# Decoder of four layers on one core: a memory region of its own for the per-token head attention, its score products in two halves, first loads and all items in another order

## The chip, the cores and the metric

The kernel runs on one core of one Trainium2 chip. The metric is the device time in microseconds (us) of one execution of the whole program. The engines are PE (TensorE, matrix products), DVE (VectorE), ACT (ScalarE), POOL (GpSimd) and SP (SyncE, which here issues all DMAs). Each works through its own list of instructions in order, and they wait for one another by semaphores.

## What is computed

A decoder of four layers with layer norm after each of its twelve stages, on x of 4 batches x 512 tokens x 128 features and a context of 154 tokens. All is float32 at the interface.

```python
x = _layernorm(x + L0_attn(x))            # 16 heads of 8, rotary, causal            stage L0a
x = _layernorm(x + L0_xattn(x, ctx))      # cross attention, 154 keys                L0x
x = _layernorm(x + L0_ffn(x))             # quantised to 8 bit, depthwise conv, silu ffn0
x = _layernorm(x + L1_attn(x))            # heads1, see below
x = _layernorm(x + L1_xattn(x, ctx, mask))#                                          L1x
x = _layernorm(x + L1_ffn(x))             # 16 experts, best two of each token       moe1
x = _layernorm(x + L2_attn(x))            # rotary, causal                           L2a
x = _layernorm(x + L2_xattn(ctx, x, mask))#                                          L2x
x = _layernorm(x + L2_ffn(x))             # 128-512-512-512-128                      ffn2
x = _layernorm(x + L3_attn(x))            # one head, distance bias                  self3
x = _layernorm(x + L3_xattn(x, ctx))      # causal                                   L3x
x = _layernorm(x + L3_ffn(x))             # 8 experts, weighted                      moe3
```

`heads1` is unusual: each token attends over its own 16 heads, not over other tokens. For each token, 16 x 16 scores are products of 8-element vectors of its query and key, a softmax runs over them, and they weigh the token's 16 value vectors of 8.

## The kernel before

Everything stays in on-chip memory with features on the partitions (`XT`, 128 x 4 x 512). The work is cut into **items**, each a (kind, stage.batch, number): `project`, `max`, `split`, `turn`, `pair`, `value`, `copy`, `out`, `mix` for the attentions with 16 heads (in two passes: `max` computes scores for the row maxima, `pair` computes them again, transposed, for exp), stage kinds such as `q0x`, `h0`, `h0t`, `h0b` (ffn0), `qkv`, `hs`, `hv`, `hm`, `ht` (heads1), `ew`, `gu`, `dn`, `acc` (experts), and the tail `wo`, `square`, `mean`, `x` that ends each stage of each batch (output product, layer norm, new x). There are 2338 items. A hand-written table `STEPS` gives the order of kinds, and three lists (`FRONT_ORDER`, `SIDE_ORDER`, `TAIL_ORDER`) the order of batches within a kind. Every engine walks through the same list `PLAN` and issues its part of each item, so the table sets the order on all five engines at once. Nothing is moved at run time: an engine whose next instruction waits does not go on to later ones.

The stages that are no 16-head attention ("side" stages: ffn0, heads1, moe1, ffn2, self3, moe3) all keep their working data in one region, `SIDE` (128 x 6656 floats). `side_free` makes the first item of each user wait for the last read of the one before, in `SIDE_ORDER`. So heads1 of a batch can't begin before ffn0 of the batch ahead of it in that list has ended, and the next ffn0 or moe1 not before `ht` of heads1.

A heads1 batch has four quarters of 128 tokens. For each, PE multiplies (`qkv`, L987), ACT copies (L1748), and DVE does `hs`: a product of 128 x 2048 elements (L1395, into `PR1`), a sum of eights (L1399), the maxima (L1400) and the subtraction (L1401). ACT takes exp (L1752). POOL does `hv`: four products of 128 x 512 (L1937, into `PV1`). DVE does `hm`: sum and reciprocal (L1405, L1406), a sum over `PV1` (L1408) and the scaling (L1409). There is one `PV1`, so `hv` of a quarter waits for `hm` of the quarter before. 

The start: SP loads the first half of the weights (`pack`), x of batch 0, the rotary tables, the constants (`STAGE`, 2496 columns), 18 small fixed rows, x of batches 1 to 3 in one transfer (L1982), then batch 0's queries and keys, which go out to DRAM (`scratch`, L2010, L2014) and come back with another layout (`QH`, `KH`, L2025). The three bf16 pieces of batch 0's queries are made by DVE (L1212 to L1216), those of its keys by POOL (L1874 to L1879). DVE casts the mask columns of the constants (L1173, in `base_setup`), and SP copies them with halves swapped into `CS` (L1988, `swap_halves`). The first `max` product on PE (L824) needs `QH`, `KH` and `CS`.

Other buffers that the change touches: `OK0` and `OK1` (normalised outputs, L1292), `OT` (turned back, the operand of `wo`), `YT` (the same for the experts), `RS0` and `RS1` (the reciprocal deviation, L1715).

## Time and profile before

| | us |
|---|---|
| median of 3 runs | 1685.9 (1683.88 to 1687.15) |
| the profiled execution, its own time | 1692.29 |
| span in its profile | 1690.6 |
| PE busy | 1359.3 (80% of the span) |
| DVE busy | 1084.9 (64%) |
| ACT busy | 736.6 (44%) |
| POOL busy | 372.9 (22%) |

Busy time is the time in which an engine has an instruction under way. Its share of the whole span says little by itself, since the stages differ: the same engine can be full in one stretch and wait in another. So the profile is read by stretches, and in each by what the waiting engines wait for. "PEclk" is the share of full TensorE speed that the chip granted: 1.00 stands for 2.4 GHz, 0.50 for 1.2 GHz.

### The profile page before, as it was taken

How to read it: one execution, taken by the hardware profiler on the slowest of the kernel's cores; microseconds unless marked ns; L12 is line 12 of the kernel's file. 1: busy time of each engine (PE TensorE's matmuls, PEld its weight loads, DVE VectorE, ACT ScalarE, POOL GpSimd, SP SyncE). 2: the span in 40 equal slices, each digit the busy share in tenths (PEclk: the TensorE clock that was granted, in tenths of full speed). 3: DMA queues.
4: the chain of work that ended last, by engine and by line, in shares of the span. 5: the costliest groups of instructions: out<-in, count | busy, mean ns of one | idle time of the engine just before them, and what ended most of it. 6: DMA issues, size and time to landing. Idle time of an engine off the chain costs nothing.

```text
span 1690.6 us, 25807 instructions
## 1 busy us (share of the span) xinstructions
PE 1359.3 (80%) x9530; PEld 648.6 (38%) x9530; DVE 1084.9 (64%) x2336; ACT 736.6 (44%) x1035; POOL 372.9 (22%) x475
## 2 busy tenths in 40 slices
PE   3476878886566676677678999899999999979986
PEld 1133433332232242244233545444444444445443
DVE  3466677887668758768987667666234624267765
ACT  1027556754323412322446653346755545435542
POOL 2214235103303312610943012022211010011000
PEclk8559899987666797799779999999999999989989
DMA  6520224200020030123113123230211321022111
GB/s 161 131 58 12 49 39 103 46 1 2 0 38 2 20 83 11 47 62 63 40 39 72 49 67 77 44 98 30 64 38 39 77 63 63 2 61 67 40 38 49
DMA packets 50072, 86.35 MB, mean 51 GB/s; under 512 B 13718, under 2 KB 42198, under 8 KB 45526
## 3 DMA queue, kind: packets, MB, share of 16 engines
q1 hardware_dynamic: 49950, 84.71, 21.7%
q8 instruction: 78, 1.28, 0.3%
q14 instruction: 44, 0.36, 0.1%
HBM read 66.95 MB, written 15.60 MB: 49 GB/s over the span
## 4 chain that ended last, share of the span: by engine, by line
PE 54%; DVE 20%; DMA 7%; ACT 6%; issue 5%; POOL 4%; SPq 4%; ACTq 0%; DVEq 0%; POOLq 0%
PE ps L897 6%; PE ps L1051 6%; PE ps L824 6%; DVE MX L1261 5%; PE ps L1017 5%; PE ps L1024 4%; PE ps L1018 4%; POOL SIDE L1937 3%; PE ps L830 3%; PE ps L735 3%; PE ps L782 3%; PE ps L858 2%; DMA SIDE<-in_experts 2%; SPq L2025 2%; ACT WORK L1683 2%
## 5 line engine op out<-in xcount | busy, mean ns | idle before, releaser
L1261 DVE TENSOR_REDUCE MX<-ps 128x3 f32<-128x462 f32 (+5 forms) x704 | 411.7, 626 | 158.0 <-PE ps L830 136.5
L1683 ACT ACTIVATE WORK<-ps 128x1024 f32<-128x1024 f32 (+1 forms) x352 | 318.8, 945 | 164.3 <-PE ps L858 122.7
L824 PE MATMUL ps<-KH,QH 48*128 48x154 bf16 (+5 forms) x1536 | 142.4, 271 | 104.5 <-DVE MX L1261 63.2
L897 PE MATMUL ps<-WORK,VA 128*18 128x512 f32 (+3 forms) x1536 | 165.7, 518 | 20.8 <-ACT WORK L1683 14.9
L1923 POOL TENSOR_SCALAR_AFFINE_SELECT WORK<-WORK 128x256 f32<-128x256 f32 (+1 forms) x192 | 95.1, 503 | 337.3 <-ACT WORK L1683 336.7
L1777 ACT ACTIVATE SIDE<-ps 128x512 f32<-128x512 f32 x96 | 57.1, 597 | 252.3 <-PE ps L1018 252.2
L1937 POOL TENSOR_TENSOR SIDE<-SIDE 128x512 f32<-128x512 f32 x64 | 113.6, 1806 | 240.3 <-ACT SIDE L1752 210.8
L824 PEld LDWEIGHTS ps<-KH,QH 48*128 48x128 bf16 (+1 forms) x1536 | 59.1, 96 | 268.2 <-DVE MX L1261 156.2
L1507 DVE TENSOR_TENSOR SIDE<-SIDE,ps 128x512 f32<-128x512 f32 x96 | 65.5, 686 | 109.1 <-ACT SIDE L1777 107.8
L858 PE MATMUL ps<-QH,KH 54*128 54x512 bf16 (+3 forms) x768 | 118.0, 352 | 19.8 <-ACT WORK L1683 17.9
L1017 PE MATMUL ps<-XT,SIDE 128*128 128x512 f32 x192 | 112.1, 668 | 20.1 <-DMA SIDE<-in_experts 19.8
L1024 PE MATMUL ps<-SIDE 128*128 128x128 f32 x768 | 110.1, 290 | 18.4 <-DVE SIDE L1507 14.9
L1024 PEld LDWEIGHTS ps<-SIDE 128*128 128x128 f32 x768 | 97.6, 198 | 49.4 <-issue 36.2
L1518 DVE SCALAR_TENSOR_TENSOR SIDE<-ps,SIDE 128x128 f32<-128x128 f32 x352 | 98.8, 343 | 18.5 <-PE ps L1024 16.5
L1018 PE MATMUL ps<-XT,SIDE 128*128 128x512 f32 x192 | 102.5, 616 | 0.0
L1876 POOL CAST HQ<-WORK 128x512 bf16<-128x512 f32 x23 | 16.0, 694 | 379.7 <-DVE WORK L1248 379.3
L782 PE MATMUL ps<-XT,pack 128*128 128x512 f32 x96 | 66.0, 796 | 23.2 <-DMA XT<-in_xT 14.5
L735 PE MATMUL ps<-pack,SIDE 128*128 128x128 f32 x260 | 50.9, 342 | 27.9 <-DVE SIDE L1384 10.3
L858 PEld LDWEIGHTS ps<-QH,KH 54*128 54x128 bf16 x768 | 33.7, 97 | 98.4 <-ACT WORK L1683 54.7
L1626 ACT ACT_TABLE_LOAD x38 | 48.8, 1283 | 30.2 <-PE ps L858 7.6
L946 PE MATMUL ps<-SQ,pack 128*128 128x512 f32 x96 | 55.1, 657 | 7.7 <-ACT SQ L1705 7.3
L897 PEld LDWEIGHTS ps<-WORK,VA 128*18 128x18 f32 x1536 | 30.2, 98 | 75.8 <-issue 29.2
(279 smaller groups left out, 2182.9 us busy)
## 6 DMA issues: line engine op xcount, KB each, us to landing
SIDE<-in_experts SPq DMA_DIRECT2D x96, 192.0 KB, 2.4
scratch<-HQ SPq DMA_DIRECT2D x48, 192.0 KB, 2.9
QH<-scratch SPq DMA_DIRECT2D x48, 192.0 KB
SIDE<-in_wide SPq DMA_DIRECT2D x8, 1024.0 KB, 6.2
QH<-scratch SPq DMA_DIRECT2D x48, 128.0 KB
scratch<-HK SPq DMA_DIRECT2D x16, 192.0 KB, 3.0
QH<-scratch SPq DMA_DIRECT2D x48, 64.0 KB
KH<-scratch SPq DMA_DIRECT2D x16, 192.0 KB
```

Of the source, the lines that this page charges most:

```text
L735: mm = pe.transpose(bank[:, t * 128:t * 128 + 128], src, eye)
L782: mm = pe.matmul(bank[:, 0:src.shape[1]], w, src, start=True, stop=True)
L824: mms[b] = pe.matmul(banks[b][:, c * pitch:c * pitch + width], qr[b][:, h, t * 128:t * 128 + 128], kr[b][:, h, 0:width], start=(c == 0), s ...
L858: mm = pe.matmul(bank[:, b, q0 * (len(hs) == 1) + i * (S - q0):][:, 0:S - q0], kr[b][:, h, kt * 128:kt * 128 + 128], qr[b][:, h, q0:S], st ...
L897: mm = pe.matmul(ps[32 * j:32 * j + 2 * NV, UB, q0:S], lhsT.rearrange("p a c -> p (a c)"), PB[:, (PAIR_BASE[F] + where[pi]) % NSLOT, b, at ...
L1017: pe.matmul(banks[:, 0, :], gates(key, i)[:, 0:128], XT[:, b, :], start=True, stop=True)
L1018: pe.matmul(banks[:, 1, :], gates(key, i)[:, 128:256], XT[:, b, :], start=True, stop=True).then_inc(all_wide, 1)
L1024: mm = pe.matmul(bank[:, t * 128:t * 128 + 128], HID[n % 2][:, t * 128:t * 128 + 128], gates(key, i)[:, 256:384], start=True, stop=True, s ...
L1051: mm = pe.matmul(bank, hidden(l, k, c), src[:, k, :], start=(k == 0), stop=(k == FC - 1))
L1261: dve.tensor_reduce(MX[:, 32 * b + i0:32 * b + i0 + cnt], src, AX.X, ALU.max, negate=True).then_inc(freed, 1)
L1683: act.activation(PB[:, N % NSLOT, :, lo:hi], wide_banks("pair", F, n)[:, :, lo:hi], ACT.Exp).then_inc(sem("exp_done"), 1)
L1937: pool.tensor_tensor(out[:, hs], SC1[i][:, hs].unsqueeze(2).broadcast_to([128, n_heads, DH, H]), v.broadcast_to([128, n_heads, DH, H]), AL ...
```

## The change

1. **A region for heads1.** `SIDE` shrinks to 5160 columns, and a new region `HEADS` (3840 columns) holds `PV1`, `QKV1`, `SC1` and `OH1`. `PR1` and two small vectors lie in `pack`, over weights of L0a and L0x that are no longer read by then (with waits for it). heads1 leaves `SIDE_USERS` and has a list of its own, so it and ffn0 or moe1 may run at the same time. `SIDE_ORDER` becomes ... heads1.0, ffn0.2, heads1.1, ffn0.3, heads1.2, moe1.0, heads1.3, moe1.1 ...
2. **Score products in halves.** `PR1` has 1024 columns in place of 2048: product and sum of eights are done for heads 0 to 7, then for 8 to 15.
3. **Memory for it.** One `OK` in place of two, `OT` in place of `YT`, the exponential of L1715 written over `SQ` in place of `RS`. The waits follow (`JOINED`).
4. **First loads.** x of batch 1 in a transfer of its own, before the constants; of the constants only the 1088 mask columns, the other 1408 later with the rest; the keys' pieces of batch 0 on DVE (`split_first`); the cast of the masks right behind it; `swap_halves` between the loads of `QH` and `KH`.
5. **Order.** All of `STEPS` is new. `TAIL_ORDER` and `FRONT_ORDER` stay.

```diff
-ffn0.0 ffn0.1 heads1.0 ffn0.2 ffn0.3 heads1.1 moe1.0 heads1.2 moe1.1 heads1.3 moe1.2 moe1.3 ffn2.0 ffn2.1 self3.0
+ffn0.0 ffn0.1 heads1.0 ffn0.2 heads1.1 ffn0.3 heads1.2 moe1.0 heads1.3 moe1.1 moe1.2 moe1.3 ffn2.0 ffn2.1 self3.0
-project*5 pieces project*5 send base max*2 pieces max*2 project max*4 project max*2 project max*3 project send max*2
+project*5 pieces send base project*5 max*2 pieces max*2 project max project max*5 project max*2 project max*2 send max
...
-        SIDE = sb("SIDE", [128, 6656])
+        SIDE, HEADS = sb("SIDE", [128, 5160]), sb("HEADS", [128, 3840])
...
-        OK = [sb(f"OK{i}", [128, QT, D]) for i in range(2)]
+        OK = sb("OK", [128, QT, D])
...
-        OT, YT = sb("OT", [128, S]), sb("YT", [128, S])
-        YC, SQ, RS = ([sb(f"{n}{i}", [128, S]) for i in range(2)] for n in ("YC", "SQ", "RS"))
+        OT = sb("OT", [128, S])
+        YC, SQ = ([sb(f"{n}{i}", [128, S]) for i in range(2)] for n in ("YC", "SQ"))
...
-        PR1, PV1 = side(0, 2048), side(2048, 2048)
+        _products = AT["L0a.wq"][0]
+        PR1, PV1 = pack[:, _products:_products + 1024], heads(0, 2048)
...
+        def heads_free(eng, key):
+            n = HEADS_USERS.index(key)
+            if n == 0:
+                consumed(eng, "rest", 0)
+                eng.wait_ge(sem("masks_ready"), 3)
+            if n:
+                filled(eng, "ht", HEADS_USERS[n - 1])
...
                 if kind == "hs":
-                    link(dve.tensor_tensor(p, qs.unsqueeze(2).broadcast_to([128, H, H, DH]),
-                                           ks.unsqueeze(1).broadcast_to([128, H, H, DH]), ALU.mult))
-                    link(dve.tensor_reduce(SC1[i], p, AX.X, ALU.add))
+                    for at in (0, HH):
+                        hs = slice(at, at + HH)
+                        link(dve.tensor_tensor(p, qs[:, hs].unsqueeze(2).broadcast_to([128, HH, H, DH]),
+                                               ks.unsqueeze(1).broadcast_to([128, HH, H, DH]), ALU.mult))
+                        link(dve.tensor_reduce(SC1[i][:, hs], p, AX.X, ALU.add))
...
                     if key == 0 and i == 1:
-                        split_queries()
+                        split_first(TQ, TRQ, HQ, (0, 1, 2), 1, "queries_split")
+                    if key == 0 and i == 3:
+                        split_first(TK, TRK, HK, (2, 1, 0), 3, "keys_split")
+                        first_masks()
...
-            sp.dma_start(STAGE, d["const"]).then_inc(sem("const_loaded"), 16)
+            sp.dma_start(XT[:, 1:2, :], d["xT"][:, 1:2, :]).then_inc(sem("x_loaded1"), 16)
+            sp.dma_start(STAGE[:, 0:NMASK], d["const"][:, 0:NMASK]).then_inc(sem("const_loaded"), 16)
...
-            sp.dma_start(XT[:, 1:B, :], d["xT"][:, 1:B, :]).then_inc(sem("x_loaded1"), 16)
+            sp.dma_start(XT[:, 2:B, :], d["xT"][:, 2:B, :]).then_inc(sem("x_loaded2"), 16)
```

Where the order moves instructions. **The start, on SP** (its list of DMAs; `QH` and `KH` are batch 0's operands, `CS` the swapped masks, `pack` at 4569 columns the second half of all weights). Before:

```order
L2025 DMA QH<-scratch 8x4096 x2
L2025 DMA KH<-scratch 24x4096 x2
L2025 DMA KH<-scratch 16x4096 x2
L2025 DMA KH<-scratch 8x4096 x2
L1963 DMA CT<-in_cT 128x640
L1964 DMA pack<-in_pack 128x4569
L1965 DMA SIDE<-in_mask_q 128x640
L1966 DMA SIDE<-in_mask_k 128x512
L1967 DMA SIDE<-in_mask_k 32x512
L1968 DMA SIDE<-in_mask_c 128x640
L1969 DMA mconst<-in_mconst 3x1
L1988 DMA CS<-const 64x1088 x2
```

Now:

```order
L2052 DMA QH<-scratch 8x4096 x2
L2015 DMA CS<-const 64x1088 x2
L2052 DMA KH<-scratch 24x4096 x2
L2052 DMA KH<-scratch 16x4096 x2
L2052 DMA KH<-scratch 8x4096 x2
L1988 DMA CT<-in_cT 128x640
L1989 DMA pack<-in_pack 128x4569
L1990 DMA SIDE<-in_const 128x1408
```

The copy into `CS` has moved from behind the load of `pack` to ahead of the loads of `KH`.

**heads1 of batch 2, on DVE.** Before, it begins when moe1 of batch 0 has ended (L1524 is that stage's `acc`, L1273 to L1276 the `split` of L1x.1):

```order
L1524 TENSOR_TENSOR YT<-ps,XT 128x512
L1261 TENSOR_REDUCE MX<-ps 128x2 x2
L1273 CAST MP<-MX 128x2x4x8
L1274 TENSOR_TENSOR MR<-MX,MP 128x64
L1275 CAST MP<-MR 128x2x4x8
L1276 TENSOR_TENSOR MP<-MR,MP 128x2x4x8
L1395 TENSOR_TENSOR SIDE<-SIDE 128x2048
L1399 TENSOR_REDUCE SIDE<-SIDE 128x256
L1400 TENSOR_REDUCE SIDE<-SIDE 128x16
L1401 TENSOR_TENSOR SIDE<-SIDE 128x256
```

Now its second quarter stands between experts of moe1.0 (L1527 is `gu`, L1536 and L1538 are `dn`, L1242 belongs to L1x.1's last projection):

```order
L1527 TENSOR_TENSOR SIDE<-SIDE,ps 128x512
L1536 TENSOR_SCALAR SIDE<-ps,SIDE 128x128 x4
L1242 TENSOR_TENSOR VR<-ps,BLOCKS 128x2x8x8
L1538 SCALAR_TENSOR_TENSOR SIDE<-ps,SIDE 128x128 x4
L1527 TENSOR_TENSOR SIDE<-SIDE,ps 128x512
L1417 TENSOR_TENSOR pack<-HEADS 128x1024
L1419 TENSOR_REDUCE HEADS<-pack 128x128
L1417 TENSOR_TENSOR pack<-HEADS 128x1024
L1419 TENSOR_REDUCE HEADS<-pack 128x128
L1420 TENSOR_REDUCE pack<-HEADS 128x16
L1421 TENSOR_TENSOR HEADS<-HEADS,pack 128x256
L1538 SCALAR_TENSOR_TENSOR SIDE<-ps,SIDE 128x128 x4
```

Two things have moved: the quarter stands ahead of fourteen of the sixteen experts of moe1.0, where it stood behind all of them, and its product and sum are each two instructions.

## Rows read from the trace of the kernel before

**Rows 1.** The page's head: busy us, share, instructions; the TensorE clock in 40 slices.

```profile
PE 1359.3 (80%) x9530; PEld 648.6 (38%) x9530; DVE 1084.9 (64%) x2336; ACT 736.6 (44%) x1035; POOL 372.9 (22%) x475
PEclk8559899987666797799779999999999999989989
```

**Rows 2.** Busy time by stretch: length, PE, PEld, DVE, ACT, POOL, PEclk, DMA share, GB/s.

```profile
57.00:393.00 336.00, 268.60 (x2414) 120.24 (x2414) 241.84 (x501) 170.86 (x249) 86.45 (x148) 0.83 0.21 44
393.00:441.00 48.00, 25.92 (x111) 7.30 (x110) 40.66 (x44) 19.25 (x29) 29.62 (x16) 0.71 0.01 2
441.00:526.00 85.00, 55.34 (x203) 29.76 (x203) 56.77 (x134) 22.13 (x36) 7.00 (x11) 0.66 0.10 19
526.00:573.00 47.00, 24.88 (x108) 6.77 (x106) 40.03 (x40) 19.49 (x29) 29.77 (x16) 0.68 0.01 2
573.00:655.00 82.00, 65.19 (x304) 35.73 (x305) 53.02 (x148) 18.45 (x29) 6.74 (x11) 0.90 0.23 58
655.00:704.00 49.00, 27.80 (x123) 9.03 (x122) 41.77 (x41) 17.45 (x25) 30.85 (x19) 0.72 0.01 2
704.00:798.00 94.00, 74.86 (x451) 41.85 (x451) 69.02 (x174) 19.53 (x30) 14.38 (x19) 0.91 0.35 77
798.00:870.00 72.00, 50.75 (x372) 16.60 (x370) 65.19 (x81) 34.05 (x47) 50.97 (x50) 0.79 0.17 35
870.00:1691.00 821.00, 751.49 (x5416) 373.61 (x5416) 460.16 (x1151) 410.86 (x557) 102.03 (x167) 0.97 0.23 54
```

**Rows 3.** The chain that ended last, in the first 60 us: start, us, what.

```profile
25.81 5.55 DMA scratch<-HQ
...
39.88 16.89 DMA CS<-const
```

**Rows 4.** Timeline of the start: start, us, engine, line, instruction, idle before it.

```profile
16.49 1.40 DVE L1244 SCALAR_TENSOR_TENSOR WORK<-ps,BROWS,tables 128x512 f32<-128x512 f32 x2
...
31.38 2.28 SPq L2025 DMA_DIRECT2D QH<-scratch  x6
...
36.39 0.43 SPq L1964 DMA_DIRECT2D pack<-in_pack  x1
...
56.96 0.61 PE L824 MATMUL ps<-KH,QH 48*128 48x512 bf16 x2 [17.85 <-DMA CS<-const]
```

**Rows 5.** Busy time by stretch of the start, with the GB/s last.

```profile
0.00:31.40 31.40, 8.35 (x19) 4.36 (x20) 11.14 (x21) 3.91 (x5) 4.99 (x9) 0.83 0.62 165
31.40:56.80 25.40, 6.04 (x20) 3.24 (x18) 5.35 (x9) 0.63 (x1) 10.09 (x10) 0.63 0.94 210
```

**Rows 6.** Timeline inside the first heads1 passage, DVE and POOL.

```profile
410.40 2.28 DVE L1395 TENSOR_TENSOR SIDE<-SIDE 128x2048 f32<-128x2048 f32 x1
410.63 7.96 POOL L1937 TENSOR_TENSOR SIDE<-SIDE 128x512 f32<-128x512 f32 x4 [2.86 <-DVE SIDE L1409]
412.72 2.29 DVE L1399 TENSOR_REDUCE SIDE<-SIDE 128x256 f32<-128x2048 f32 x1
415.50 1.74 DVE L1401 TENSOR_TENSOR SIDE<-SIDE 128x256 f32<-128x256 f32 x1
418.69 2.29 DVE L1408 TENSOR_REDUCE SIDE<-SIDE 128x128 f32<-128x2048 f32 x1 [0.84 <-POOL SIDE L1937]
```

**Rows 7.** By line: all instructions of L1395, L1401 and L1937, ns min/median/max.

```profile
L1395 DVE TENSOR_TENSOR SIDE<-SIDE x16: 2282/2292/3417, 394.0 to 845.4; 128x2048 f32<-128x2048 f32 x16
L1401 DVE TENSOR_TENSOR SIDE<-SIDE x16: 424/1386/1790, 399.1 to 850.5; 128x256 f32<-128x256 f32 x16
L1937 POOL TENSOR_TENSOR SIDE<-SIDE x64: 1464/1503/3598, 400.2 to 858.7; 128x512 f32<-128x512 f32 x64
```

**Rows 8.** Who waited for whom, from 238 to 256 us: us in total, times, longest.

```profile
PE ps L782 <- DVE XT L1316: 5.7, 1, 5.7
```

**Rows 9.** Timeline of POOL, splitting queries and keys of L1x.1: first and last instruction.

```profile
594.37 0.61 POOL L1876 CAST HQ<-WORK 128x512 bf16<-128x512 f32 x1 [23.43 <-DVE WORK L1248]
...
602.30 0.31 POOL L1905 CAST MK<-MKF 3x160 bf16<-3x160 f32 x1
```

More of the change, by code:

```diff
@@ L217, in stage_items @@
     elif stage == "ffn2":
-        add("wide", 0, x if b else x + [("x", ("L0x", B - 1), 0), ("x", ("ffn0", B - 1), 0)])
+        add("wide", 0, x if b else x + [("x", (other, B - 1), 0) for other in ("L0x", "ffn0", "heads1")])
         if b == 0:
@@ new lines @@
+value*2 pair max pair copy wo max value send max square pair mean max value x max pair split project value pair*2 turn
+max value max pair project pair out value max value*2 max value copy pair max pair out project*2 pieces pair max mix
+pair*2 max value pair max wo pair square pair max value max pair tables2 value max pair*2 send split value pair*2 turn
+pair value*3 pair value copy pair mean value pair w0 pair value pair masks max x pair value pair*2 max project pair
+project value pair max value*3 max pair value copy max pair out pair max value max pair out pair max value max pair
@@ L444 @@
 TAIL_OF = {key: n for n, key in enumerate(TAILS)}
-TURNED = [key for kind, key, i in PLAN if kind in ("mix", "ht")]
-SUMMED = [key for kind, key, i in PLAN if kind == "acc"]
-SIDE_USERS = [key for kind, key, i in PLAN if not isinstance(key, int) and (kind, i) == FIRST.get(key[0])]
+JOINED = [(kind, key) for kind, key, i in PLAN if kind in ("mix", "ht", "acc")]
+SIDE_USERS = [key for kind, key, i in PLAN if not isinstance(key, int) and (kind, i) == FIRST.get(key[0]) and key[0] != "heads1"]
+HEADS_USERS = [("heads1", b) for kind, (stage, b), i in ITEMS if stage == "heads1" and (kind, i) == FIRST[stage]]
 def stage_end(stage):
@@ L467, in check_plan @@
             assert where[("x", TAILS[n - 2], 0)] < where[("wo", key, 0)], key
-    for n, key in enumerate(TURNED[1:]):
-        kind = "mix" if isinstance(key, int) else "ht"
-        assert where[("wo", TURNED[n], 0)] < where[(kind, key, 0)], key
+    for n, (kind, key) in enumerate(JOINED[1:]):
+        assert where[("wo", JOINED[n][1], 0)] < where[(kind, key, 0)], key
     for kind in ("pair", "value", "copy", "out", "project", "max", "split", "turn", "send", "mix"):
@@ L1282, in normalise @@
                 rd = RD[:].rearrange("p (n a b) -> p n a b", a=2, b=2)
-                if u == 0 and F >= 2:
-                    filled(dve, "mix", F - 2)
+                if u == 0 and F:
+                    filled(dve, "mix", F - 1)
                 if 2 * F + u:
```

238 lines of the change are left out of this document (121 added, 117 removed).

## Prediction

> **What bounds the kernel now.** I read first the page's head and its clock line, then busy time by stretch, then the chain that ended last for the start, and then the timeline inside the stretches that looked odd. The head alone says "PE, 80%" [rows 1], but its clock line has fives and sixes in two places: the first 100 us and the stretch from about 400 to 850 us. The table by stretch shows why they differ from the rest [rows 2]. From 870 us to the end PE is busy 751 of 821 us (92%) at a clock of 0.97: that half is bound by PE. From 393 to 870 us, 477 us in seven stretches, PE is busy 324.7 us (68%) at 0.66 to 0.91, and DVE 366.5 us (77%; the sum of the seven DVE columns). Four of the seven are passages in which a batch of heads1 runs (393 to 441, 526 to 573, 655 to 704, 798 to 870). In the first three, DVE is busy 122.5 of 144 us, 85%, and PE little more than half; in the stretches between them DVE is at 65 to 73%. So DVE's work stands in lumps there: too much in the passages, where PE starves, too little between them. And the start ends with the first score product at 56.96 us, held for 17.85 us by one transfer alone [rows 4].
>
> **The start (point 4 of the change).** The chain waits for the queries to be written to `scratch` until 25.81 + 5.55 = 31.4 us [rows 3]. Then `QH` is issued, `KH` behind it, and the transfer into `CS`, issued behind `pack`, takes until 39.88 + 16.89 = 56.8 us [rows 3, 4]. All of this is queueing: up to 31.4 us the transfers move 165 GB/s, and from there to 56.8 us 210 GB/s [rows 5]. So I count bytes.
> Removed ahead of the queries: 1408 columns x 128 x 4 bytes = 0.72 MB, which at 165 GB/s is 4.4 us. x of batches 1 to 3 is the same amount in two transfers. The queries are written at 31.4 - 4.4 = 27.0 us.
> Behind them come `QH` 0.79 MB, `CS` 0.28, `KH` 0.79 and the keys going out, 0.39: 2.25 MB, at 210 GB/s 10.7 us, so the first product is at 37.7 us, where 56.96 stood. Saved: **19 us**. DVE's own list has to be ahead of that, and it is: splitting keys, casting masks and centring follow on the keys' projection, which ended by 17.9 us [rows 4], and are some 6 us by estimate, and batch 1's projections then still have over 10 us. The bounds: 21 us if the keys' writing overlaps fully, 7 us if the operands come no earlier than 50 us since small rows queue worse than their bytes say. I take 19, because both rates are of this very queue. What comes next is late by nothing that I can see: batch 1's operands now sit behind `pack` and 0.72 MB more, but they are wanted only after batch 0's 22 pairs of maxima.
>
> **heads1 in a region of its own (points 1 and 5).** The work stays the same in kind, so the gain is what DVE's idle time between the lumps can take. In halves, an `hs` costs more. From a product of 2048 elements at 2.292 us and one of 256 at 0.424 us [rows 7], an element costs 1.04 ns and an instruction 0.157 us whatever its size. One more product and one more sum, with two more gaps of 0.04 us between instructions [rows 6], are 0.39 us, times 16 quarters: 6.3 us on DVE, with no cover, as it is the fuller engine there. DVE's work in the 477 us becomes 366.5 + 6.3 = 372.8 us.
> What share can DVE reach? The floor is today's 77%, the passages reach 85%, and the last passage, where maxima of L2a run beside heads1, 65.19 of 72 us, 91% [rows 2]. The midpoint between 77 and 85 is 81, that between 77 and 91 is 84. I take 82%, nearer to the first, because three of the four passages are at 85 and because ffn0's chain of small steps between PE, DVE and ACT remains. 372.8 / 0.82 = 455 us, so **22 us** less than 477. The bounds: at 88%, 424 us, 53 us less; at 77.5%, 481 us, 4 us more.
> The gain rests on who is late next. In 573 to 655 and 704 to 798 us PE is busy 65.19 and 74.86 us of 82 and 94 [rows 2], and a quarter of heads1 placed between experts makes DVE late for an expert's product: PE, two products ahead, covers one such lump of 5.5 us but not two. That too is why I don't take 88%.
>
> **Two engines on one port.** In the first passage DVE's 2048-element product starts at 410.40 us, POOL's four products at 410.63, and POOL takes 7.96 us for what is 4 x 1.50 = 6.0 us at the median; then DVE's subtraction of 256 elements takes 1.74 us, where it takes 0.42 undisturbed [rows 6, 7]. Each engine holds the other up when both read two operands from on-chip memory.
> The Trainium skill states this as a rule ("SBUF — State Buffer", section "Who interferes with whom"): a DVE instruction with two SBUF inputs and a GpSimd instruction that reads SBUF exclude one another for a whole instruction. The trace agrees (1.74 against 0.42 us). It speaks against splitting the product, and by it each of 16 quarters could wait once more; taken at its full, as in the first rival below, it would give 1671 in place of 1645.
> Priced from the rows: at most 16 x (1.79 - 0.42) = 21.9 us more on DVE, at least nothing, since POOL too is now held by a product half as long. I leave it at nothing in the sum, and its upper end is part of a rival.
>
> **The rest.** One `OK`, one `OT` for both uses, and the exponential in place add waits, but each on a step that the old order too had finished: a batch's `mix` stands ahead of the next batch's `out` in both lists, and the tails are in the same sequence. Nothing, with 2 us as the upper bound. Where the old order put DVE's setup of ffn0's weights (`w0`) ahead of x of L0a.1, PE waited 5.7 us for it [rows 8]; in the new one `w0` and the masks stand ahead of x of L0a.2, so I move that wait and don't remove it: 0, between 5.7 less and 3 more. `rest`, with its long run on ACT, stays in its place. In the last 821 us PE is 92% busy, and its list differs only in detail: 0, give or take 6.
> **Sum.** 19 + 22 = 41 us. The profiled execution takes 1692.3 us, so it would take 1651. The runs' median is 6.4 us below that execution: 1685.9 - 41 = **1645 us**.
>
> **The rivals.**
> *The middle gives nothing* (1667 to 1673 us). For it: DVE's new products cost 6.3 us, and where a half waits for POOL, up to 21.9 more; (372.8 + 21.9) / 0.82 = 481 us, 4 us longer than now, so 1685.9 - 19 + 4 = 1671. Nor does moving work help if DVE's waits are for chains (product, exp, POOL, sum) and not for lack of work. Against it: in the passages DVE is idle 0.8 us before L1408 in each quarter [rows 6], little to wait for, and it is PE that starves.
> *DVE fills up* (1614 us). 88% gives 53 us: 1685.9 - 19 - 53. For it: 91% is reached in one passage, and PE's clock of 0.66 to 0.72 in the passages could rise as its gaps close, which takes PE out of the way. Against it: no other stretch between 393 and 870 is above 85%.
> *The start is held by something else* (1657 us): operands only at 50 us, 7 in place of 19. For it: `KH` still comes last in the queue. Against it: the rates of rows 5.
> *Slower* (1701 us). POOL's list is in order, and in the new order the first `hv` of heads1.2 stands behind L1x.1's split, as before, but now DVE's `hm` of the same quarter follows after some 13 us of DVE work, while POOL needs 594.37 to 602.6, 8.2 us, for that split [rows 9] and 6 to 8 for `hv`: DVE would wait up to 3.5 us at that spot. If every one of the 16 quarters had such a wait, it would be 56 us: 1685.9 - 41 + 56 = 1701. It decides from 41 / 16 = 2.6 us a quarter. Against it: in most quarters the new order leaves other work of DVE between `hv` and `hm`, and I found four places at most where a split of POOL stands between.
>
> **How the numbers follow.** The forecast as worked out (1645) 0.45; the middle gives nothing 0.2; DVE fills up 0.15; a start held 0.1; slower 0.05; the rest, 0.05, is spread over the range. The range takes in the start held and the middle without gain, with 3 us for the late part, and on the other side the filled DVE at its centre: **1612 to 1676 us**. Outside it are the slower case and half of the fullest one. A measurement of this kernel can tell about 0.2% (3.4 us) from no change. Faster by more than that: 0.92; within it: 0.03; slower: 0.05.
>
> **What would show it.** The first L824 at 36 to 40 us, and no wait of PE for `CS`. POOL's `hv` as four times four separate groups spread over the time in place of blocks of 43 us; from the first `qkv` of heads1 to the last `hm`, DVE's share at 82% and PE's clock higher than 0.7. A median of L1401's successor above 1.4 us, or halves of the product far above 1.22 us, would mean the port. The forecast is wrong if DVE's share there stays below 79%, if the first product comes after 45 us, or if the last half of the kernel moves by more than 6 us.

## The result, and the profile after

| | before | changed |
|---|---|---|
| median of the runs | 1686.5 us (1683.9 to 1690.3) | 1625.4 us (1620.3 to 1631.7) |
| profiled execution | 1692.3 us | 1625.4 us, its span 1623.7 |
| ratio | | 0.9634, 95% interval 0.9601 to 0.9667 |

The changed kernel is 61 us faster, where 41 were forecast. The time lies inside the range, but neither of the two terms has its size: the start gave less, the middle much more. The page after, to be laid beside [rows 1]:

```profile
span 1623.7 us, 25862 instructions
...
PE 1325.5 (82%) x9530; PEld 634.5 (39%) x9530; DVE 1093.8 (67%) x2373; ACT 743.0 (46%) x1040; POOL 363.7 (22%) x470
...
PEclk8688899997768789898899998999999999989999
```

The two fives of the first 100 us became a six and an eight, and of the three sixes between about 420 and 550 us one is left.

**Where the time went.** VectorE writes a batch's new x at the end of each of its twelve stages, 48 times in all. These instants are marks that can be laid side by side. They are starts of L1316 before, of L1331 after (us):

| x of | before | after | moved | start alone (e1) |
|---|---|---|---|---|
| L0a.0 | 211.9 | 184.0 | -27.9 | -15.3 |
| L0x.0 | 314.8 | 301.1 | -13.8 | -12.8 |
| ffn0.2 | 567.6 | 517.3 | -50.2 | -15.9 |
| heads1.2 | 722.1 | 665.4 | -56.6 | -17.2 |
| heads1.3 | 874.4 | 801.5 | -72.8 | -19.5 |
| the last, moe3.3 | 1683.4 | 1616.5 | -66.9 | -24.8 |

The rows of the marks that bound the middle, from the timelines of VectorE, before and after:

```profile
314.83 0.68 DVE L1316 TENSOR_TENSOR XT<-YC,RS 128x512 f32<-128x512 f32 x1
...
874.36 0.68 DVE L1316 TENSOR_TENSOR XT<-YC,RS 128x512 f32<-128x512 f32 x1
```

```profile
301.07 0.68 DVE L1331 TENSOR_TENSOR XT<-YC,SQ 128x512 f32<-128x512 f32 x1
...
801.53 0.68 DVE L1331 TENSOR_TENSOR XT<-YC,SQ 128x512 f32<-128x512 f32 x1
```

From x of L0x.0 to x of heads1.3, which is called the middle from here on, 559.5 us became 500.5: 59 us less. What comes before it is 13.8 us shorter. What comes after it is 6 us longer in this execution, and 0.4 us shorter (1617.8 - 801.9 = 815.9 us against 816.2) in another execution of the same kernel, e9. So the last half changed by no more than two executions of one kernel differ. (e1's profiled execution is one of its shorter ones, a span of 1665.7 us at a median of 1674.8, so its marks drift ahead towards the end.)

**The middle.** Busy time by stretch (columns as in [rows 2]: length, PE, PEld, DVE, ACT, POOL, PEclk, DMA share, GB/s), before:

```profile
315.00:874.00 559.00, 390.68 (x2068) 176.74 (x2060) 431.05 (x811) 197.65 (x288) 169.33 (x141) 0.80 0.14 31
874.00:1690.00 816.00, 748.14 (x5384) 372.30 (x5380) 456.94 (x1145) 408.21 (x554) 102.03 (x167) 0.97 0.23 55
```

and after:

```profile
301.00:802.00 501.00, 357.56 (x2022) 167.45 (x2018) 436.27 (x841) 196.51 (x285) 164.81 (x141) 0.84 0.16 35
802.00:1623.00 821.00, 751.18 (x5426) 370.21 (x5426) 459.56 (x1148) 414.25 (x560) 102.59 (x167) 0.97 0.23 54
```

VectorE's work is almost the same, 436.3 against 431.1 us, and its share rose from 77% to 87%. TensorE's busy time fell by 33 us for about the same matmuls, with the granted clock at 0.84 in place of 0.80. What VectorE waited for in the middle shrank from 116 to 51 us in all: for ACT from 55 to 23 us, for TensorE from 56 to 26, for POOL from 5 to 2. The largest single wait, for the activation of an expert ahead of `gu`, before and after (us in all, times, longest):

```profile
DVE SIDE L1507 <- ACT SIDE L1777: 41.0, 29, 8.7
```

```profile
DVE SIDE L1527 <- ACT SIDE L1801: 21.8, 20, 3.1
```

POOL's groups of `hv` show what the order did. They stood 2.86 us apart, in blocks of four; now other work lies between them (timeline of POOL, three of sixteen):

```profile
388.21 7.96 POOL L1962 TENSOR_TENSOR HEADS<-HEADS 128x512 f32<-128x512 f32 x4 [12.88 <-DVE HEADS L1429]
400.78 5.91 POOL L1962 TENSOR_TENSOR HEADS<-HEADS 128x512 f32<-128x512 f32 x4 [4.61 <-DVE HEADS L1429]
417.18 5.90 POOL L1962 TENSOR_TENSOR HEADS<-HEADS 128x512 f32<-128x512 f32 x4 [10.48 <-DVE HEADS L1429]
```

**The start.** The chain that ended last, at the beginning (start, length, what), answers to [rows 3]:

```profile
6.50 0.44 SPq L2007
...
15.22 3.22 SPq L2007
18.49 1.82 SPq L2008
...
22.76 0.70 SPq L2037
23.51 5.06 DMA scratch<-HQ
28.59 0.32 SPq L2052
...
34.34 12.34 DMA KH<-scratch
46.67 0.35 issue
47.03 0.61 PE ps L834 x2
```

And the two stretches that answer to [rows 5]:

```profile
0.00:28.50 28.50, 12.97 (x29) 6.85 (x30) 17.00 (x33) 3.91 (x5) 0.20 (x4) 0.83 0.56 157
28.50:47.00 18.50, 2.12 (x10) 1.17 (x10) 1.50 (x2) 0.63 (x1) 9.59 (x10) 0.68 0.97 161
```

The wait for `CS` is gone, but `KH` takes its place at the end: the first score product stands at 47.03 us, not at 37.7. From the queries' writing at 28.6 us to the first product, 18.4 us at 161 GB/s are 2.96 MB, where the forecast counted 2.25 MB at 210: another 0.71 MB travelled beside them.

### The profile page after: what moved, and what is told of

The parts are those of the page before. It is cut to its first block, busy times and chain, and to the rows that moved or that the text cites. A ratio compares the mean times of both kernels' runs of the same rounds, so it can differ in the third digit from the quotient of the medians.

```text
span 1623.7 us, 25862 instructions
## 1 busy us (share of the span) xinstructions
PE 1325.5 (82%) x9530; PEld 634.5 (39%) x9530; DVE 1093.8 (67%) x2373; ACT 743.0 (46%) x1040; POOL 363.7 (22%) x470
## 4 chain that ended last, share of the span: by engine, by line
PE 50%; DVE 25%; DMA 6%; issue 6%; ACT 5%; SPq 4%; POOL 3%; ACTq 0%; DVEq 0%; POOLq 0%
PE ps L907 6%; PE ps L1061 6%; PE ps L834 5%; DVE MX L1276 5%; PE ps L1027 4%; PE ps L1028 4%; PE ps L1034 4%; PE ps L840 3%; DMA KH<-scratch 3%; PE ps L868 2%; DVE pack L1417 2%; PE ps L792 2%; DVE HEADS L1419 2%; SPq L2052 2%; DMA scratch<-HQ 2%
## 5 line engine op out<-in xcount | busy, mean ns | idle before, releaser
L1276 DVE TENSOR_REDUCE MX<-ps 128x3 f32<-128x462 f32 (+5 forms) x704 | 412.0, 627 | 144.1 <-PE ps L840 119.9
L834 PE MATMUL ps<-KH,QH 48*128 48x154 bf16 (+5 forms) x1536 | 139.0, 266 | 112.8 <-DVE MX L1276 61.7
L1962 POOL TENSOR_TENSOR HEADS<-HEADS 128x512 f32<-128x512 f32 x64 | 106.0, 1689 | 241.7 <-DVE HEADS L1429 133.8
L1527 DVE TENSOR_TENSOR SIDE<-SIDE,ps 128x512 f32<-128x512 f32 x96 | 65.6, 686 | 94.1 <-ACT SIDE L1801 93.9
L1538 DVE SCALAR_TENSOR_TENSOR SIDE<-ps,SIDE 128x128 f32<-128x128 f32 x352 | 98.9, 343 | 17.6 <-PE ps L1034 15.2
L956 PE MATMUL ps<-SQ,pack 128*128 128x512 f32 x96 | 55.6, 663 | 13.7 <-ACT SQ L1729 12.8
L792 PE MATMUL ps<-XT,pack 128*128 128x512 f32 x96 | 58.3, 718 | 5.9 <-DVE XT L1331 4.3
L1331 DVE TENSOR_TENSOR XT<-YC,SQ 128x512 f32<-128x512 f32 x48 | 36.4, 759 | 35.6 <-ACT SQ L1739 35.5
L1325 DVE SCALAR_TENSOR_TENSOR YC<-ps,BO,XT 128x512 f32<-128x512 f32 x28 | 20.9, 747 | 57.8 <-PE ps L930 32.4
```

The lines of the kernel that those rows point to most:

```text
L834: mms[b] = pe.matmul(banks[b][:, c * pitch:c * pitch + width], qr[b][:, h, t * 128:t * 128 + 128], kr[b][:, h, 0:width], start=(c == 0), s ...
L1276: dve.tensor_reduce(MX[:, 32 * b + i0:32 * b + i0 + cnt], src, AX.X, ALU.max, negate=True).then_inc(freed, 1)
L1538: ins = dve.scalar_tensor_tensor(out=o, in0=p, scalar=s, in1=o, op0=ALU.mult, op1=ALU.add)
L1962: pool.tensor_tensor(out[:, hs], SC1[i][:, hs].unsqueeze(2).broadcast_to([128, n_heads, DH, H]), v.broadcast_to([128, n_heads, DH, H]), AL ...
```

## The experiments

Twelve runs were made, e9 among them with the changed kernel itself. Each time below is a median. Its ratio is to the kernel before, run beside it.

### The start alone

e1: the kernel before with point 4 of the change and nothing else. The core of the edit, all of it as in the change:

```
-project*5 pieces project*5 send base max*2 ...
+project*5 pieces send base project*5 max*2 ...
-            sp.dma_start(STAGE, d["const"])...
+            sp.dma_start(XT[:, 1:2, :], d["xT"][:, 1:2, :])...
+            sp.dma_start(STAGE[:, 0:NMASK], d["const"][:, 0:NMASK])...
+                    if key == 0 and i == 3:
+                        split_first(TK, TRK, HK, (2, 1, 0), 3, "keys_split")
+                        first_masks()
```

> The kernel before with point 4 alone (x of batch 1 first, constants in two loads, VectorE splitting the first keys, CS issued between QH and KH); heads1, its products and the whole later order as before. Theory A, the start is worth what its first product moved, 10 us (56.96 to 47.03), and the rest of the 61 us comes from the middle: first score product at 47 us, time 1676 to 1678 us. Rival B, the start is a part of the larger gain because everything behind it follows a better fed PE, the 19 us of the forecast: 1667 us. Rival C, nothing, because the later order waits at the same places: 1686 us.

Measured: 1674.8 us, ratio 0.9927 (0.9898 to 0.9957), so 12 to 13 us of the 61; its first score product at 47.3 us. Theory A holds, with about 3 us more than the product itself moved (9.6 us). They may lie in TensorE's clock right behind it. The first 38 us from the first product on, before and in e1:

```profile
57.00:95.00 38.00, 26.12 (x160) 11.74 (x160) 25.55 (x43) 0.63 (x1) 9.57 (x10) 0.50 0.24 47
```

```profile
47.00:85.00 38.00, 24.13 (x209) 12.55 (x210) 27.95 (x47) 0.64 (x1) 9.58 (x10) 0.68 0.48 134
```

Before, the lower of the clock's two levels (1.2 GHz, 0.50) lay over the whole stretch. In e1 it was 0.68, more matmuls fit into it, and x of L0a.0 came 15.3 us earlier, not 9.6. A part of that was given back by L0x.0. How much of it is the edit isn't settled: this clock also differs between executions of one kernel, 0.54 to 0.68 with an unchanged start (see "The first loads").

### Region and halves without the order

e2: the changed kernel with the old tables `STEPS` and `SIDE_ORDER`; only the first items stand as in the change, so that its start is the same as e1's.

```
-ffn0.0 ffn0.1 heads1.0 ffn0.2 heads1.1 ffn0.3 heads1.2 moe1.0 heads1.3 ...
+ffn0.0 ffn0.1 heads1.0 ffn0.2 ffn0.3 heads1.1 moe1.0 heads1.2 moe1.1 heads1.3 ...
```

> The changed kernel with the old order of all items (only the first items in the new form, so that the start is the new one): region of its own for heads1, products in halves, one OK, one OT. Theory A, the region gives nothing by itself, it only permits the order: 1686.5 less 10 of the start plus 6.3 of the split products on a full VectorE, 1683 us, and heads1's passages still hold VectorE at 85% and POOL's products in four blocks. Rival B, the region ends waits of heads1 and ffn0 for each other's buffers and so brings the middle's gain with any order: under 1650 us. Rival C, the halves relieve the port: the small sums behind them shrink from 1.39 to 0.43 us and it ends at 1670 us or less.

Measured: 1680.2 us, ratio 0.9952 (0.9926 to 0.9977). Beside e1 that is 5 us more (the intervals overlap), and 55 us above the changed kernel. Theory A: the region in itself gives nothing. The other half of the question has no run: no kernel has a new order with the old region, so how much of the 55 us an order alone could give isn't known. The middle of e2:

```profile
302.00:858.00 556.00, 396.43 (x2070) 179.07 (x2064) 432.07 (x844) 198.07 (x288) 168.16 (x141) 0.78 0.14 31
```

VectorE at 78%, as before. The halves were expected to put 6.3 us on VectorE, but its busy time is only 1.0 us above the one before. Two groups of lines show why (busy us, mean ns):

```profile
L1418 DVE TENSOR_TENSOR pack<-HEADS 128x1024 f32<-128x1024 f32 x32 | 42.1, 1316 | 1.7 <-ACT HEADS L1773 1.1
...
L1422 DVE TENSOR_TENSOR HEADS<-HEADS,pack 128x256 f32<-128x256 f32 x16 | 14.5, 908 | 0.5
```

and the same before:

```profile
L1395 DVE TENSOR_TENSOR SIDE<-SIDE 128x2048 f32<-128x2048 f32 x16 | 39.1, 2441 | 1.1 <-ACT SIDE L1748 1.0
...
L1401 DVE TENSOR_TENSOR SIDE<-SIDE 128x256 f32<-128x256 f32 x16 | 18.3, 1141 | 0.5
```

The products cost 3.0 us more and the sums 2.4 (39.0 against 36.6 us in all), but the subtraction behind them 3.8 less. Why the subtraction shrank isn't tested here; beside POOL's products it is the instruction that had been held up [rows 6], so the port is the likely reason, and it gave back part of the split's price where a loss was feared.

### heads1 together again

e5: the reverse test. All is as changed, only the sixteen steps of each batch of heads1 are moved back to one another. In `STEPS`, around the second batch:

```
-h0b project h0t project h0b hs pieces hv wo send q0x max q0t max square max hm h0 hv h0 qkv silu0 qkv max*4 silu0 max*2
-silu0*2 max*2 split h0t turn h0t pair h0b*2 hs h0t pair*2 value pair*2 hm h0t value pair*2 value h0b pair hv h0b copy
...
+h0b pieces wo send q0x max q0t max square max h0*2 silu0 max*4 silu0 max*2 silu0*2 max*2 split h0t turn h0t pair h0b qkv
+h0b h0t qkv hs pair*2 value hv pair hs hm qkv hv pair h0t value pair hs pair hm value hv qkv h0b pair h0b copy mean
```

> The changed kernel with the steps of heads1 alone moved together again: in each batch the sixteen steps qkv, hs, hv and hm stand as far ahead of their ht as in the old order (48, 48, 52 and 112 items in place of 78, 96, 128 and 215); all other steps, the region, the start and the halves as in the changed kernel. Theory A, the gain of the middle comes from spreading heads1's work over VectorE: VectorE's share between x of L0x.0 and x of heads1.3 falls from 87% to 80% or less and the time rises by 35 us or more, to 1660 to 1680. Rival B, the gain comes from the rest of the searched order (ffn0 and the experts among the attention's items), and spreading is only one part: 1630 to 1645 us.

Measured: 1709.9 us, ratio 1.0151 (1.0103 to 1.0198): 84 us above the changed kernel and slower than the kernel before. Its middle:

```profile
305.00:884.00 579.00, 372.70 (x2026) 172.61 (x2022) 429.93 (x841) 202.01 (x290) 161.92 (x141) 0.81 0.14 31
```

The same work of VectorE (429.9 us), 78 us longer, a share of 74%. That is more than theory A gave. Rival B falls: without the spreading, nothing of the rest of the order helps. That it ends above the kernel before also shows the limit of this test. The order was searched as a whole, and what stands around the lump was placed for a spread heads1. That spreading is what fills VectorE is in line with e5, but not shown apart from the rest: 84 us is the price of breaking the order at this place, not the sum that spreading alone would bring to the old order.

### More work on VectorE, more on TensorE

e4 puts work on VectorE in the middle, e6 on TensorE:

```
-        PR1, PV1 = pack[:, _products:_products + 1024], heads(0, 2048)
+        PR1, PV1 = pack[:, _products:_products + 512], heads(0, 2048)
...
-                    p = PR1.rearrange("p (h g e) -> p h g e", h=HH, g=H)
-                    for at in (0, HH):
-                        hs = slice(at, at + HH)
+                    p = PR1.rearrange("p (h g e) -> p h g e", h=4, g=H)
+                    for at in range(0, H, 4):
+                        hs = slice(at, at + 4)
...
```

> The changed kernel, with the score products of heads1 in four parts of 512 elements in place of two of 1024: two more products and two more sums a quarter, by 0.157 us fixed and 0.04 us of gap each 0.79 us, times 16 quarters 12.6 us more on VectorE, all in the middle. Theory A, VectorE at 87% is now the bound of the middle, so this comes through in full: 1638 us (12 to 14 more). Rival B, VectorE and PE wait for each other in turn and the order has slack: 3 to 7 us more. Rival C, shorter products are less held up by POOL (a small gain against the cost): 0 to 3 us more.

```
                     bank = ring(kind, key, i)
+                    pe.matmul(bank[:, 0:384], XT[:, b, i * 128:i * 128 + 128], W("L1a.wqkv"), start=True, stop=True)
                     pe.matmul(bank[:, 0:384], XT[:, b, i * 128:i * 128 + 128], W("L1a.wqkv"), start=True, stop=True)\
```

> The changed kernel with each of heads1's 16 projections computed twice into the same bank: two more passes of 0.486 us on TensorE each, 15.6 us in all, in the middle and nothing on VectorE. Theory A, VectorE at 87% sets the middle's length and TensorE at 71% has room: 0 to 5 us more, 1625 to 1630. Rival B, the two wait for each other in turn, so that work on either comes through: 12 us more or above, 1637 or more.

Measured: e4 1642.9 us (ratio 0.9743, 0.9672 to 0.9815), 17.5 us more than the changed kernel (its interval alone is 12 us wide to either side, but the middle of the trace is longer by the same 17.5); e6 1626.2 us (0.9649, 0.9601 to 0.9697), no difference that can be measured. The middle of e4, then of e6:

```profile
306.00:824.00 518.00, 363.49 (x2016) 170.71 (x2015) 449.89 (x904) 196.34 (x285) 159.02 (x141) 0.82 0.15 34
```

```profile
304.00:806.00 502.00, 367.30 (x2048) 174.07 (x2046) 436.39 (x840) 196.33 (x285) 164.84 (x141) 0.84 0.16 35
```

In e4 VectorE has 13.6 us more to do (12.6 were worked out), its share stays at 87%, and 13.6 / 0.87 = 15.6 of the 17.5 us follow. In e6 the 32 added passes took 0.486 us each at the median, 15.6 us; TensorE's whole busy time rose by 9.7, and the middle is 1.5 us longer, where two executions of the changed kernel differ by 0.6. Theory A in e6, and in e4 too, with 17.5 us where 12 to 14 were expected.

### Less work on VectorE

e11 leaves out heads1's guard against large scores, the maximum of a row and its subtraction:

```
-                        link(dve.tensor_reduce(SC1[i][:, hs], p, AX.X, ALU.add))
-                    link(dve.tensor_reduce(MH1[i], SC1[i], AX.X, ALU.max))
-                    dve.tensor_tensor(SC1[i], SC1[i], MH1[i].unsqueeze(2).broadcast_to([128, H, H]), ALU.subtract)\
+                        ins = dve.tensor_reduce(SC1[i][:, hs], p, AX.X, ALU.add)
+                        if at == 0:
+                            link(ins)
+                    ins.then_inc(sem("scores1_shifted"), 1)
```

> The changed kernel without the step of heads1 that finds each row's maximum and subtracts it ahead of the exponential (a quotient of sums of exponentials is the same without it, as long as no score is large; the guard against large scores is what is left out). On VectorE 16 sums at 0.42 and 16 subtractions of 11.0 us in all, with their gaps 18.7 us, go from the middle. Theory A, VectorE bounds the middle at a share of 87% in either direction: 18.7 / 0.87 = 21 us less, 1604 us. Rival B, VectorE binds upward only, and TensorE with its 71% at a clock of 0.84 comes next: 5 to 10 us less, 1615 to 1620.

> The changed kernel itself, unaltered, so that the three kernels beside it can be compared with it on one chip: 1625 us, ratio 0.963 to the kernel before.

Measured: e11 1616.7 us (0.9581, 0.9547 to 0.9615), the changed kernel beside it, e9, 1623.0 us (0.9634, 0.9601 to 0.9668). That is 6 us less, not 21. The middle of e11:

```profile
301.00:795.00 494.00, 362.45 (x2022) 171.38 (x2022) 418.42 (x807) 197.01 (x286) 164.15 (x143) 0.83 0.17 36
```

VectorE has 17.9 us less to do, and the middle is 6.8 us shorter (by the marks 302.5 to 796.2, 493.7 us against 500.5; against e9's 501.1 it is 7.4). Its share falls to 85%. Rival B: VectorE holds the middle against more work, but once its work shrinks, something else ends the waits for more than half of the time. The trace of e11 says for the most part what: VectorE's waits in the middle add up to 63 us, where the changed kernel has 51, and of the 12 us more, 9 are waits for TensorE (35 against 26), the rest for ACT and POOL. So rival B's guess that TensorE comes next is right as to the waits. It isn't TensorE's sheer work, since e6 raised that for nothing; that the fixed order places these products late is the likely reason, which no run tests.

### The first loads

In the changed kernel VectorE has the last piece of the queries ready at 16.25 us, but SyncE sends them out only at 22.76, behind its eighteen issues of fixed rows. Most of them take 0.44 to 0.80 us, three in the middle 1.7 to 3.2: one takes 0.44 us at 6.50, and the same one 3.22 us at 15.22 (chain above). The row from VectorE's timeline:

```profile
15.56 0.69 DVE L1226 TENSOR_TENSOR HQ<-WORK,HQ 128x512 bf16<-128x512 f32 x1
```

So two causes were named for the first product at 47 us, and taken away one by one. e3 issues later what nobody needs yet (x of batches 2 and 3, and all of `load_rest`):

```
-            sp.dma_start(XT[:, 2:B, :], d["xT"][:, 2:B, :]).then_inc(sem("x_loaded2"), 16)
...
                     load_operands(key)
                     if key == 0:
+                        sp.dma_start(XT[:, 2:B, :], d["xT"][:, 2:B, :]).then_inc(sem("x_loaded2"), 16)
+                    if key == 1:
                         load_rest()
```

e7 does so with the fixed rows of two of the three operand buffers, where `fixed_rows(i)` holds the six transfers of buffer i:

```
-            for i in range(3):
...
+            fixed_rows(0)
...
                     load_operands(key)
+                    if key == 0:
+                        fixed_rows(1)
+                        fixed_rows(2)
                     if key == 0:
                         load_rest()
```

e8 does both, and e10 both, except that x of batches 2 and 3 keeps its early place.

> The changed kernel, with x of batches 2 and 3 loaded behind the first operands and the context, the second part of the weights, the rest of the constants and the masks behind batch 1's operands. Theory A, transfers queued beside KH delay it: from 28.6 to 47.0 us 161 GB/s moved 2.96 MB where QH, CS, KH and the outgoing keys are 2.25 MB, so the other 0.71 MB cost 4.4 us. First product at 42.6 us, time 4 us under the changed kernel's, 1621. Rival B, the small rows of QH and KH are themselves slow and the others only filled gaps: first product within 1 us of 47.0, time 1625. Rival C, what is put off is late for batch 1 or for the context's projections: a later wait eats it, 1625 or more although the first product is earlier.

> The changed kernel with the twelve transfers that fill fixed rows of operand buffers 1 and 2 issued behind batch 0's operands. In the trace VectorE has the queries' pieces ready at 16.5 us, but SyncE sends them out only at 22.0, behind eighteen issues of fixed rows of which some take 1.4 to 3.2 us. Theory A, SyncE's list holds the start: with six issues ahead the queries go out at 16.5 to 17.5 us and the first score product comes 5 us earlier, 42 us; time 1620. Rival B, the queue's bytes hold the start: twelve transfers more beside KH, first product at 46 to 48 us, 1625.

> Both delays together: fixed rows of buffers 1 and 2 and x of batches 2 and 3 behind batch 0's operands, the context, the second part of the weights, the rest of the constants and the masks behind batch 1's. Theory A, the two are different queues (SyncE's list, the transfers' bytes) and add: first product at 35 to 36 us and 1612 to 1614 us. Rival B, they overlap, or batch 1's operands become late once batch 0 starts this early (they went out from 32.6 us on): first product earlier, but L0a.1 not, 1618 us or above.

> The changed kernel with the fixed rows of operand buffers 1 and 2 behind batch 0's operands and the context, the second part of the weights, the rest of the constants and the masks behind batch 1's; x of batches 2 and 3 in its early place again. In the run with both delays TensorE waited at 44.2 us for x of batch 2, and in all three runs with an earlier first product its clock stood at 0.50 to 0.59 from the first product to about 80 us, where it was 0.63 to 0.72 in the changed kernel. Theory A, the wait for x goes (first product at 39 to 40 us), but the slow clock takes back more than half of the 7 to 8 us: 1618 to 1621 us. Rival B, only the wait for x stood in the way: 1614 us or less.

The clock in the last column is that of the 38 us from the first product on:

| | median, ratio (95%) | first score product | x of L0a.0 | PEclk behind the first product |
|---|---|---|---|---|
| changed | 1625.4, 0.9634 (0.9601 to 0.9667) | 47.0 | 184.0 | 0.68 |
| e9, the same again | 1623.0, 0.9634 (0.9601 to 0.9668) | 47.1 | 186.5 | 0.59 |
| e11, start unchanged | 1616.7, 0.9581 (0.9547 to 0.9615) | 45.9 | 185.5 | 0.59 |
| e3 | 1618.9, 0.9607 (0.9542 to 0.9672) | 41.1 | 182.5 | 0.50 |
| e7 | 1618.9, 0.9600 (0.9552 to 0.9649) | 41.2 | 181.9 | 0.54 |
| e8 | 1620.2, 0.9618 (0.9572 to 0.9665) | 37.3 | 179.0 | 0.54 |
| e10 | 1614.9, 0.9586 (0.9554 to 0.9618) | 38.1 | 179.5 | 0.50 |
| e12, e7's start in e11 | 1609.6, 0.9553 (0.9516 to 0.9589) | 38.1 | 178.9 | 0.54 |

The first cause, SyncE's list, is shown: in e7, e8, e10 and e12 the queries go out at about 16 us and the first product comes 6 us or more earlier. In e10 the queries go out as soon as they are ready, and `KH` takes 9.5 us in place of 12.3 (chain that ended last):

```profile
16.28 0.70 SPq L2043
17.03 5.43 DMA scratch<-HQ
...
28.23 9.51 DMA KH<-scratch
```

The second cause, bytes beside `KH`, is shown less well. In e3 the first product comes 6 us earlier (4.4 were expected), of which 2.2 lie in the writing of the queries, ahead of which x of batches 2 and 3 no longer stands, and 3.0 in `KH`, 9.4 us in place of 12.3. But e7 and e12 have the same edit of the start, with all of `load_rest` early, and `KH` takes 12.2 us in e7 and 9.7 in e12. So `KH` differs by as much between two executions, and on top of the late fixed rows the late `load_rest` brings nothing that can be told apart: 38.1 us in e10, 38.1 in e12.

How much of the gain reaches x of L0a.0? The six executions with the changed kernel's start (changed, e4, e5, e6, e9, e11) have their first product at 45.9 to 47.1 us, a clock of 0.54 to 0.68 behind it and x of L0a.0 at 184.0 to 189.1, 186.3 in the middle; the changed kernel's own has the highest clock and the earliest x. Against 186.3, x comes 4 us earlier in e3 and e7, and 7 us in e8, e10 and e12, so most of the gain does arrive. The stretch behind the first product, in e9 and in e10:

```profile
47.00:83.00 36.00, 23.95 (x160) 10.73 (x160) 25.40 (x43) 0.63 (x1) 9.59 (x10) 0.59 0.47 137
```

```profile
37.00:80.00 43.00, 28.83 (x207) 14.21 (x208) 27.75 (x46) 0.63 (x1) 10.46 (x11) 0.50 0.60 146
```

In e10 the engine had been idle for 8.7 us ahead of the first product, in e9 for 17.9, and yet the clock stays at its lower level for 43 us. From the first product to x of L0a.0 e10 needs 141.4 us and e9 139.4: 2 of the 9 us won in waiting are paid back there. In e8 TensorE also waited at 44.2 us for x of batch 2, which e10 loads early again:

```profile
44.20 2.08 PE L792 MATMUL ps<-XT,pack 128*128 128x512 f32 x2 [1.03 <-DMA XT<-in_xT]
```

In the medians e3, e7 and e8 stand 5 to 6.5 us under the changed kernel with intervals that overlap its own, so only their direction can be named. Theory A of e3 and of e7 fits, in the first product and in the time. Of e8 neither theory fits: 1620.2 us and not 1612 to 1614, though x of L0a.1 does come earlier (214.7 us in place of 219.7). e10 and e9 ran side by side: 1614.9 against 1623.0, 8 us or 0.5%, the intervals (0.9554 to 0.9618 and 0.9601 to 0.9668) overlapping by a little. e10 computes all that the changed kernel computes and has the lowest median of those that do. Its theory A fails, since far less than half was taken back; the time, just above rival B's 1614, is nearer to rival B.

e12 joins the late fixed rows of e7 with e11:

> The kernel without the subtraction of the maximum and with the fixed rows of buffers 1 and 2 issued late: the two lie in different stretches and add. Theory A: 1625 less 21 less 6, 1598 us. Rival B, the shorter chain of the start is taken back once the middle is shorter, or the middle's gain is half of it: 1608 us or more.

Measured: 1609.6 us (0.9553, 0.9516 to 0.9589), 13.4 under e9: 6.4 of e11 and 7.1 of the start. The two parts add, but since the middle's part is a third of what theory A gave it, the total lies near rival B's. Beside e11, the late fixed rows alone give 7.1 us here, almost the 8.1 of e10 over e9 with both changes.

## Why the prediction was right in its range and wrong in its terms

The time fell into the range, 20 us below the forecast, and partly by luck: the start was put 9 us too high at the first product and the middle 37 us too low, and the two errors offset each other in part.

**What bounds the kernel** was read rightly: VectorE in lumps in the middle, TensorE behind 870 us, one transfer at the start. e4, e5 and e6 show it for the middle. The last part, 0 give or take 6, holds, at its edge in one execution: 816.2 us before, 822.2 after and 815.9 in e9.

**The start: 19 us forecast, 10 at the first product, 12 to 13 in the time.** The step that failed is "all of this is queueing", with its count of bytes. The queries were written at 28.6 us and not 27.0, since they waited for SyncE's list (1.6 us). The trace before shows that wait already: the queries were ready at 16.6 us and SyncE came to them at 23.9.

```profile
15.88 0.69 DVE L1216 TENSOR_TENSOR HQ<-WORK,HQ 128x512 bf16<-128x512 f32 x1
```

```profile
23.89 1.87 SPq L2010
```

So taking 4.4 us of bytes off ahead of them moved them by 2.8 only, and with the list shortened too (e7) they were written at 22.9 us. The 2.25 MB came at 161 and not 210 GB/s: 14.0 us and not 10.7 (3.3 us). And 0.71 MB that were issued around them were left out of the sum: 4.4 us. 37.7 + 1.6 + 3.3 + 4.4 = 47.0. This splits the difference up; that the 0.71 MB cost 4.4 us isn't shown, since e12 came to 38.1 us with them in the queue. The rate was carried over from a stretch with another mix of transfers, and of the traffic in the queue only the part was counted that is waited for. The prediction had named this reading as a rival (operands at 50 us, 7 us). The condition "wrong if the first product comes after 45 us" was met, and so the start has to be called wrong, though the total was not.

**The middle: 22 us forecast, 59 measured.** The form of the sum was right and its share wrong. Put on the stretch between the marks: (431.1 + 6.3) us of work before, divided by the measured share of 0.871, gives 502 us; measured were 500.5. With the 0.82 of the forecast it would be 533. The step that failed is the choice of 82% between rows at 77, 85 and 91%. It lets the new order fill VectorE less than three of the passages before did, with "one such lump TensorE covers but not two" as a reason. The measured 87% lies between the passages' 85%, which would have given 45 us, and the 91% of the passage in which other work ran beside heads1, which would have given 79; 88%, the rival's share, was nearest. That rival (53 us of the middle) is what happened there.

**The split products: 6.3 us forecast, 1 to 5 measured.** In VectorE's busy time 1.0 us (e2), in the medians of e1 and e2 5 us, with intervals that overlap. In the changed kernel products, sums and subtractions together take 94.9 us, where they took 94.0.

**The port.** The forecast left it at nothing. The subtraction, behind the sums and the maximum, now takes 0.43 us at the median, where it took 1.39 [rows 7]; both stand here for the changed kernel:

```profile
L1417 DVE TENSOR_TENSOR pack<-HEADS 128x1024 f32<-128x1024 f32 x32 | 44.9, 1402 | 0.6
...
L1421 DVE TENSOR_TENSOR HEADS<-HEADS,pack 128x256 f32<-128x256 f32 x16 | 11.0, 685 | 0.5
```

The subtraction went from 18.3 to 11.0 us in all, the products from 39.1 to 44.9, against 2 x 16 x 1.22 = 39.0 undisturbed. So the clash has moved more than it has gone: where a product meets POOL it still pays. Set against undisturbed times (an estimate from 2.292, 1.22 and 0.424 us an instruction, and 0.69 for a product of 512 elements), products and subtractions paid 14 us to it before, 10 in the changed kernel, and 17 in e4, where the subtraction is down to 7.5 us and the products are up to 60.6. That POOL is the cause is read from such places, not tested by a run without POOL's products. The timeline has such a place, with POOL's four products from 367.23 us on:

```profile
367.23 8.11 POOL L1962 TENSOR_TENSOR HEADS<-HEADS 128x512 f32<-128x512 f32 x4 [67.06 <-ACT HEADS L1776]
...
369.04 2.41 DVE L1417 TENSOR_TENSOR pack<-HEADS 128x1024 f32<-128x1024 f32 x1
371.48 1.22 DVE L1419 TENSOR_REDUCE HEADS<-pack 128x128 f32<-128x1024 f32 x1
372.74 1.23 DVE L1417 TENSOR_TENSOR pack<-HEADS 128x1024 f32<-128x1024 f32 x1
```

The rule of the Trainium skill ("SBUF — State Buffer", section "Who interferes with whom") is in line with this: the product with two on-chip inputs takes 2.41 us in place of 1.23, the sum with one input behind it its usual 1.22. The second product, at 372.74 us with POOL's group still under way, took 1.23, and that group took 8.11 us, where others took 5.9.

**"Slower", since `hm` waits for POOL** did not come: VectorE's wait for POOL ahead of `hm` is 2.0 us in all 16 quarters together, where it was 5.1. (That was six waits of at most 0.9 us; the forecast read one of 0.8 us "in each quarter". Nor do the sixes of the clock line reach to 850 us: they end at about 550.)

```profile
L1428 DVE TENSOR_REDUCE HEADS<-HEADS 128x128 f32<-128x2048 f32 x16 | 36.6, 2286 | 2.5 <-POOL HEADS L1962 2.0
```

**The rest** at nothing is in line with the last half, and with x of L0x.0, where the changed kernel (-13.8) and the start alone (-12.8) stand almost together.

## What to carry to other kernels

When an order is opened up so that one engine's work can be spread, the work divided by the share that this engine will reach gives the time. Here that share (87%) lay between the engine's own fullest passages (85%) and the one passage in which other work ran beside it (91%), not halfway back to the average of 77%. Ask of a transfer that is waited for what else is in the queue beside it, needed or not, and at what instant the issuing engine can issue it at all: here an engine had the data ready 6 us before its turn in the list. And compare such small gains with several executions of the same kernel: here the clock behind the first product alone differed from 0.54 to 0.68 with an unchanged start, and x of L0a.0 by 5 us.

## What the hardware showed that was not expected

- TensorE's granted clock stood at its lower level for 43 us behind the first product in e10 (0.50, engine busy 28.8 of 43 us), at 0.68 in e1 and 0.50 in the kernel before (38 us each), with 160 to 209 matmuls in the stretch. In six executions with one and the same start it was 0.54 to 0.68. The idle time ahead of it doesn't separate these cases (17.9 us before at 0.50, 18.4 in e1 at 0.68, 17.9 in e9 at 0.59, 8.7 in e10 at 0.50), so it stays open what does.
- The issue of a small transfer of fixed rows took 0.44 us for the first ones, 3.22 us for the fifth of its kind, and 0.49 for the last; with six in place of eighteen fixed rows ahead, the first product came 6 us (e7) and 8 us (e12 beside e11) earlier.
- The same queue moved 161 GB/s in one stretch at a DMA share of 0.97 and 210 at 0.94 [rows 5]: a high share does not tell the rate.
- Work added to the bounding engine cost 1.3 times its size (13.6 us, 17.5 in the time), work taken from it gave about a third (17.9 us, 6.4): more and less work did not cost and give alike.
